# First attention's value products of two head groups at once on four 64x64 quadrants

## What is computed

```python
def _L0_attn_ref(x, q_weight, v_weight, out_w, out_b):
    q = jnp.einsum('tbm,mhd->tbhd', x, q_weight)
    q_sq = jnp.einsum('tbhd,tbhd->tbh', q, q)
    squared_dist = q_sq[:, None] + q_sq[None, :] - 2.0 * jnp.einsum('tbhd,sbhd->tsbh', q, q)
    attn_weights = jax.nn.softmax(-squared_dist * inv_sqrt_d, axis=1)
    A = jnp.einsum('mhd,nhd->hmn', q_weight, q_weight) * inv_sqrt_d
    XA = jnp.einsum('tbm,hmn->tbhn', x, A)
    PXA = jnp.einsum('tsbh,sbhm->tbhm', attn_weights, XA)
    PXAV = jnp.einsum('tbhm,mhd->tbhd', PXA, v_weight).reshape(x.shape[0], x.shape[1], -1)
    return PXAV @ out_w.T + out_b
...
x = x + _L0_attn_ref(_layernorm(x, axis=-1), ...)
x = x + _L0_ffn_ref(_layernorm(x, axis=-1), ...)
```

## Time and profile before

| what | us |
|---|---|
| median of 3 runs (570.55 to 576.7) | 572.35 |
| profiled execution, whole time | 571.84 |
| profiled execution, span of the core | 570.1 |
| PE busy in the span | 563.5 |
| DVE, POOL, ACT busy | 342.5, 230.2, 204.9 |

### The profile page before, as it was taken

How to read it: one execution, slowest core, us unless ns; L and a number is a source line. 1 busy time by engine, 2 the same in 40 slices (tenths; PEclk the granted TensorE clock), 3 DMA queues, 4 the chain that set the end, 5 groups by cost and what they waited for, 6 DMA issues and landing times.

```text
span 570.1 us, 11756 instructions
## 1 busy us (share of the span) xinstructions
PE 563.5 (99%) x5017; PEld 484.4 (85%) x5019; DVE 342.5 (60%) x386; ACT 204.9 (36%) x296; POOL 230.2 (40%) x182
## 2 busy tenths in 40 slices
PE   9999999999999999999999899999999999999997
PEld 6989898898989989898778898978888888888886
DVE  4878672736637265562687467476585447867741
ACT  4543443505335250442562361423341122434220
POOL 2399995674727557368035001103335443000000
PEclk9999999999999999999999999999999999999999
DMA  8463534241222323105240420206923222699501
GB/s 309 144 220 104 180 127 156 75 156 47 100 83 84 146 74 94 62 1 155 59 149 3 160 77 1 75 1 151 229 75 131 91 74 75 186 236 234 156 1 74
DMA packets 24852, 64.91 MB, mean 114 GB/s; under 512 B 2408, under 2 KB 2408, under 8 KB 21872
## 3 DMA queue, kind: packets, MB, share of 16 engines
q1 hardware_dynamic: 24816, 64.38, 36.1%
HBM read 63.20 MB, written 1.18 MB: 113 GB/s over the span
## 4 chain that ended last, share of the span: by engine, by line
PE 89%; DVE 1%; DMA 1%; issue 0%; ACT 0%; POOL 0%
PE ps L333 18%; PE ps L335 18%; PE ps L334 18%; PE ps L864 9%; PE ps L887 3%; PE ps L891 3%; PE ps L879 2%; PE ps L874 2%; PE ps L873 2%; PE ps L878 2%; PE ps L941 2%; PE ps L1187 1%; PE ps L905 1%; DMA raw<-in_ctx 1%; PE ps L912 1%; PE ps L1170 1%
## 5 line engine op out<-in xcount | busy, mean ns | idle before, releaser
L473 POOL TENSOR_TENSOR psum_tmp<-psum_tmp,raw 128x512 f32<-128x512 f32 (+1 forms) x88 | 147.7, 1679 | 28.7 <-DVE lo L1431 20.0
L864 PE MATMUL ps<-hi 128*128 128x256 f32 (+3 forms) x416 | 129.2, 312 | 0.1
L1431 DVE TENSOR_TENSOR lo<-raw,hi 128x2048 fp32r<-128x2048 f32 (+1 forms) x29 | 62.3, 2166 | 30.9 <-ACT hi L545 30.8
L864 PEld LDWEIGHTS ps<-hi 128*128 128x128 f32 (+1 forms) x416 | 78.2, 188 | 1.7 <-DVE lo L1431 0.4
L333 PE MATMUL ps<-hi,gh 128*128 128x512 f32 x192 | 75.5, 393 | 0.0
L335 PE MATMUL ps<-hi,gl 128*128 128x512 f32 x192 | 74.8, 390 | 0.0
L334 PE MATMUL ps<-lo,gh 128*128 128x512 f32 x192 | 74.7, 389 | 0.0
L526 POOL TENSOR_TENSOR sx<-sx,raw 128x512 f32<-128x512 f32 x32 | 41.1, 1290 | 78.2 <-DVE raw L1779 78.1
L749 ACT ACTIVATE hi<-raw 128x2048 fp32r<-128x2048 f32 x14 | 26.8, 1916 | 87.2 <-PE ps L335 77.6
L333 PE MATMUL ps<-wvh,gh 128*128 128x512 f32 x128 | 51.1, 400 | 0.0
L335 PE MATMUL ps<-wvh,gl 128*128 128x512 f32 x128 | 50.0, 391 | 0.0
(11 more groups left out here) (229 smaller groups left out, 1168.2 us busy)
## 6 DMA issues: line engine op xcount, KB each, us to landing
raw<-in_ctx SPq DMA_DIRECT2D x23, 1024.0 KB, 4.9
raw<-in_ve SPq DMA_DIRECT2D x8, 1024.0 KB, 5.3
raw<-in_oe SPq DMA_DIRECT2D x8, 1024.0 KB, 7.1
wk<-gm_rows SPq DMA_DIRECT2D x8, 512.0 KB, 9.7
g<-gm_rows SPq DMA_DIRECT2D x8, 512.0 KB, 10.6
raw<-in_ctx SPq DMA_DIRECT2D x8, 130.0 KB
xres<-in_x SPq DMA_DIRECT2D x1, 1024.0 KB, 9.7
mb<-in_WqT SPq DMA_DIRECT2D x1, 1024.0 KB, 13.6
```

The lines of the kernel that those rows point to most:

```text
L473: pool.tensor_tensor(psum_tmp[0:k, :], (raw[:, 0, :] if t == 1 else psum_tmp[0:k, :]), raw[0:k, t, :], ALU.add).then_inc(ctx_sum, 1)
L864: pe.matmul(dst, hi[0:kk, t, cols], x, start=start and opens, stop=stop and closes, skip_group_check=True)
L1431: dve.tensor_tensor(lo[0:k, r, :], raw[0:k, r, :], hi[0:k, r, :].bitcast(F32), ALU.subtract).then_inc(ctx_lo, 1)
```

## The change

`near_values(n, gs)` now does the head groups 2n and 2n+1 together. The odd one's output goes to the other 64 rows, so that it uses the two quadrants off the diagonal. Its rows are therefore swapped by halves through `near_norm`, and its transposes multiply by a permutation, `swapped`, in place of the identity. POOL makes `swapped` in three instructions. `near_norm(0)` takes its two banks one after the other. Three orders are rewritten: PE's products, ACT's fourth values ahead of its fourth exponential, and DVE's two low parts for the next layer, which go behind `near_low(3)`.

```diff
@@ POOL, behind masks()
+            pool.memset(swapped[:, :], 0.0).then_inc(swap_set, 1)
+            for n, base in enumerate((S, -S)):
+                pool.wait_ge(swap_set, n + 1)
+                pool.affine_select(out=swapped[:, :], in_=swapped[:, :], compare_op=ALU.not_equal, fill=1.0, base=base,
+                                   pattern=[[-1, P]], channel_multiplier=1).then_inc(swap_set, 1)
@@ ACT
             nearness(2)
+            values_out(3)
             nearness(3)
-            values_out(3)
@@ PE
-            def near_values(c, gs=range(NG)):
-                pe.wait_ge(d_exp, c + 1)
+            def near_values(n, gs):
+                pe.wait_ge(d_exp, 2 * n + 2)
...
-                    pe.wait_ge(vv_done, g + 1 if c != 1 or g < 2 else NG)
+                    pe.wait_ge(vv_done, g + 1 if g < 2 else NG)
                     for j in range(4):
...
+                        for turned in range(2):
+                            c = 2 * n + turned
+                            for cg in range(2):
+                                row = slice(S * cg, S * cg + S)
+                                out_row = S * (1 - cg if turned else cg)
+                                col = (g % 2) * 4 + j
+                                mm = pe.matmul(bank[num_bank(c, g)][out_row:out_row + S, col * (D1 + 1):(col + 1) * (D1 + 1)],
...
-                    mm.then_inc(nv_mm, 1)
+                    mm.then_inc(nv_mm, 2)
...
-                    mm = pe.transpose(turn_bank(c)[:, tok], mb[:, c, tok], ident[:, :])
+                    mm = pe.transpose(turn_bank(c)[:, tok], mb[:, c, tok], (ident, swapped)[c % 2][:, :])
@@ DVE
-            w_low(W_Q2, 0)
             near_norm(0)
             near_norm(1)
             near_norm(2)
             near_low(0)
             near_low(1)
-            dve.wait_ge(wg_hi_done, 2)
-            dve.tensor_tensor(wg_lo, wg_raw, wg_hi.bitcast(F32), ALU.subtract).then_inc(wg_lo_done, 1)
             near_norm(3)
             near_low(2)
             near_low(3)
+            w_low(W_Q2, 0)
+            dve.wait_ge(wg_hi_done, 2)
+            dve.tensor_tensor(wg_lo, wg_raw, wg_hi.bitcast(F32), ALU.subtract).then_inc(wg_lo_done, 1)
```

More of the change, by code:

```diff
@@ L86, in perceiver_block @@
         identb = sb("identb", [P, P], BF16)
+        swapped = sb("swapped", [P, P])
         headmask = sb("headmask", [P, P])
@@ L151, in perceiver_block @@
         ld_w = [sem("ld_w0"), sem("ld_w1")]
-        consts, bfconst, blank_set = sem("consts"), sem("bfconst"), sem("blank_set")
+        consts, bfconst, blank_set, swap_set = (sem(s) for s in ("consts", "bfconst", "blank_set", "swap_set"))
         c_mm, c_done, ld_bq = sem("c_mm"), sem("c_done"), sem("ld_bq")
@@ L1171, in head_values @@
                 mm.then_inc(vv_mm, 1)
-            def near_values(c, gs=range(NG)):
-                pe.wait_ge(d_exp, c + 1)
-                if c == 0:
+            def near_values(n, gs):
+                pe.wait_ge(d_exp, 2 * n + 2)
+                if n == 0:
                     pe.wait_ge(vv_ones, 1)
                     pe.wait_ge(row_done, 2)
-                if c == 2:
+                else:
                     pe.wait_ge(d_add, 8)
                 for g in gs:
-                    pe.wait_ge(vv_done, g + 1 if c != 1 or g < 2 else NG)
+                    pe.wait_ge(vv_done, g + 1 if g < 2 else NG)
@@ L1183, in near_values @@
                     for j in range(4):
[L1184 to L1189, removed]
+                        for turned in range(2):
[5 more added lines that the diff above has]
+                                mm = pe.matmul(bank[num_bank(c, g)][out_row:out_row + S, col * (D1 + 1):(col + 1) * (D1 + 1)],
+                                               near_heads_of(c)[row, j * 2 * P + g * S:j * 2 * P + g * S + S],
+                                               vv[row, g, 4 * c + j, :], start=True, stop=True, skip_group_check=True)
@@ L1190, in near_values @@
                 if gs.stop == NG:
-                    mm.then_inc(nv_mm, 1)
+                    mm.then_inc(nv_mm, 2)
             def turn_values(c):
                 pe.wait_ge(nv_done, c + 1)
+                if c == 1:
+                    pe.wait_ge(swap_set, 3)
                 for g in range(NG):
                     tok = slice(g * P, (g + 1) * P)
-                    mm = pe.transpose(turn_bank(c)[:, tok], mb[:, c, tok], ident[:, :])
+                    mm = pe.transpose(turn_bank(c)[:, tok], mb[:, c, tok], (ident, swapped)[c % 2][:, :])
@@ L1210, in _ @@
             near_values(0, range(0, 2))
+            head_values(3)
+            near_values(0, range(2, NG))
             near_values(1, range(0, 2))
-            head_values(3)
-            near_values(2, range(0, 2))
-            near_values(0, range(2, NG))
             near_values(1, range(2, NG))
-            near_values(2, range(2, NG))
             turn_values(0)
             turn_values(1)
-            near_values(3)
             def transpose_e(u):
@@ L1669, in near_norm @@
                 dve.wait_ge(nv_mm, c + 1)
[L1670 to L1674, removed]
+                parts_of = range(2) if c == 0 else range(1)
+                count = 2 // len(parts_of)
+                steps = 2 if c == 0 else c + 2
+                for n in parts_of:
+                    heads = ps[:, num_bank(c, 2 * n):num_bank(c, 2 * n) + count, 0:8 * (D1 + 1)].rearrange("p k (h d) -> p k h d", d=D1 + 1)
+                    per_head = rowrec[:, c, :].rearrange("p (k h) -> p k h", k=2)[:, n:n + count, :]
+                    dve.reciprocal(per_head, heads[:, :, :, D1]).then_inc(d_rec, 1)
+                    dve.wait_ge(d_rec, n + 1 if c == 0 else steps)
+                    ins = dve.tensor_tensor(mb[:, c, :].rearrange("p (k h d) -> p k h d", k=2, d=D1)[:, n:n + count, :, :], heads[:, :, :, 0:D1],
+                                            per_head.unsqueeze(3).broadcast_to([P, count, 8, D1]), ALU.mult)
+                ins.then_inc(nv_done, 1)
             def near_low(c):
```

## The result

| | before | changed |
|---|---|---|
| median of 20 runs, us | 573.01 | 575.74 |
| lowest and highest, us | 570.55, 579.05 | 571.48, 579.21 (of 19) |
| profiled execution, whole time and span, us | 571.84, 570.1 | 578.5, 576.8 |
| granted clock of PE over that span, mean | 1.00 | 0.99 |

The ratio is 1.0045 (95% interval 1.0023 to 1.0066): slower by about half a per cent. The forecast was 571.1, with a range up to 574.2, so it missed, and its sign too. One of the 20 changed runs took 3156 us: the ratio and the highest time leave it out, the median has it in and is 575.63 without it.

What follows compares the result with a forecast made beforehand. PE was taken as the bound, busy 563.5 of 570.1 us. Of 3.6 us saved on the value products, new waits left a lead of 0.68: 571.84 less 0.7 gives 571.1 us, range 568.9 to 574.2.

Steps and rivals of the forecast that it cites:

- Points 1 and 2: First two quarters of the value products: the first ends at 334.08, the second waits 0.68 us for the values' copy.
- the first rival: Value products: the four quadrants do not overlap, 31 ns per instruction, nothing saved, 574.7 us; chance 0.11.
- The copy's wait: Ahead of the second quarter of value products: PE newly waits 0.68 us for ScalarE's copy of the last values.
- The gross saving: Value products: 256 instructions at 17.0 ns instead of 31.1, 3.6 us.
- Point 3: Last two quarters of value products: the fourth exponential costs PE nothing, 0.1 us to spare; both end at 339.12.
- Points 4 to 8: Norms to transposes: out_part(0) waits 0.96 us, PE gets 1.83 ahead, VectorE only 0.32, transposes wait about 0.9.
- The waits at the transposes: Layer norm's transposes ahead of the second layer: PE waits about 0.9 us for VectorE's second tile.
- The last rival: Ahead of the change, at L335: the 1.6 us stall repeats or is lost, 572.7 or 569.5 us; chance 0.06.

Runs made afterwards that it cites:

- e1: The changed kernel run again with no edit, against the kernel before: 575.49 us, ratio 1.0086.
- e3: The changed kernel with 96 more PE instructions at its start (four large and 53 very small warm-up products for nine): 573.81 us, ratio 1.0052 to the kernel before.
- e7: The changed kernel with the load of W_K2 held until the second row of norms is done: 575.32 us, ratio 1.0035 to the kernel before.
- e13: The changed kernel with W_K2's load later and the last values computed ahead of the first quarter of products: 572.19 us, ratio 0.9993 to the kernel before.
- e5: The changed kernel with 96 more PE records at its start, eight of nine large warm-up products kept: 572.99 us, ratio 0.9998 to the kernel before.
- e9: The kernel before with only the load of W_K2 made later: 570.80 us, ratio 0.9945 to the kernel before.
- e11: The changed kernel with W_K2's load later and 14 extra products on zeros filling PE's pauses: 574.52 us, ratio 1.0023 to the kernel before.
- e12: The changed kernel with W_K2's load later, 12 filling products and VectorE's low parts at their old places: 576.99 us, ratio 1.0061 to the kernel before.
- e14: The changed kernel with W_K2's load later, last values first, low parts back, first expert's load held: 571.00 us, ratio 0.9988 to the kernel before.

## Why the prediction was wrong

**Points 1 and 2 held.** 64 instructions took 1.07 us (forecast 1.09), 16.7 ns each against 31, so the four quadrants do overlap and the first rival is out. What the prediction drew for that rival from the Trainium skill's page TensorE: Matmul & The Clock Gate, Part 3 (The mechanism), that four quadrants with two row groups go no faster than two, does not hold in these products either. The copy's wait was 0.78 (0.68). The gross saving was put at 3.6 us, all 256 instructions at 31.1 ns; the earlier trace rows have 7.83 us for them, which makes it 3.5. The walk through the points goes by the rows and is not touched by this.

**Point 3 failed: "Both quarters end at 339.12".** It counted 128 instructions at 17 ns behind the second quarter and asked for nothing but semaphores. PE's instructions have to arrive, too. In e1, the run at full clock, the quarters ended 8.04 us after the first began (333.77 to 341.81), not 6.13, and 1.83 of the difference of 1.91 is the stall for the piece at record 7445. From the first product to the queries e1 took 24.16 us, before 22.74, and the forecast says 22.06. The fourth exponential, of which point 3 was afraid, made no wait.

**Points 4 to 8 held, about 2 us late.** out_part waited 1.07 us (0.96); VectorE went from `near_low(3)` without a break to the residual, which came 16.88 us after the first product in e1 and 15.18 in before: 1.70 later, where 0.32 earlier was forecast. The waits at the transposes were 0.5 in all (0.9). In e3, where the stall was 0.48, the first product to the queries took 22.80 us, 22.74 before; less the stall that is 22.3, against 22.06 by the forecast.

**The clock was taken as 1.00 throughout**, because the profiled execution showed nothing else. The runs shown already reached 576.7; the scatter of 6 us was put down as scatter, and it was the clock's falls. With the change they came in 21 of 23 runs instead of 44 of 110. By the sessions' medians a run with a fall takes 4.4 us more (571.0 against some 575.4). An estimate from these numbers is (0.91 - 0.40) x 4.4 = 2.2 of the 2.7 us between the two medians. It leaves +0.5 where the forecast had -0.7; that this is the stall is argued, from the traces, since only two runs of the changed kernel were at full clock (571.48 and 574.19). **The last rival was near**: a stall that "a changed instruction stream might repeat". It was the right place to look, but priced as chance, at 0.06, and without its mechanism, which makes it repeat where the products use up a piece before the next one has come.

What stays open: which pauses bring the clock down. No order by the longest or the summed pause of the traces fits: e7 (0.97, 0.78, 0.62 and 0.65) fell in 8 of 10, e13 (1.02, 1.84 and 1.07) in 4 of 10, e5 (0.76, 0.78 and 1.06) in none, and e1's traced execution had 0.71, 0.78, 1.83 and 1.07 without a fall. e9 and e11 show that the falls go away with the pauses: with the stall near 324 us in before, with work put into them in the changed stretch. How many or how long they must be is not shown, and neither is where e11's other runs lost their 2 us.

## What to carry to other kernels

When a change makes many short instructions run faster, ask how fast they can be delivered: here 256 records (a product instruction is two, with its weight load) take 3.6 to 3.9 us to come, so less than about 15 ns per record, kept up over more than one piece, was not to be had. A stall marked "issue" with no releaser, at a fixed record number, is a sign of such a piece. A large load moving at that time makes it longer, and one wait on SyncE can move the load away; but look where it moves to, since here it held up a later piece. And read the spread of the runs before the forecast: a spread of 1% on one core was here a second mode, and a change that adds pauses can move runs into it.

## What the runs showed of the hardware that I had not expected

- Between 320 and 365 us the stalls without a releaser fall on a grid of 256 PE records (6677, 7189, 7445, 7701) in every kernel traced. Where PE stalled with no 1 MB load in the way, 3.3 us (e11: 335.56 to 338.85) to 4.1 us (e13: 334.62 to 338.72) had passed from PE's start in one piece, or from the end of a semaphore's wait among its first ten records, to the first record of the next.
- A 1 MB load in flight made that 6.0 us (e12: 336.72 to 342.75). The piece then moved in the load's last microsecond: 323.23 and 323.41 in before, 331.48 and 331.77 in e14, 340.23 and 340.46 in e12 (start of the packet, end of the load).
- The granted clock went to 0.5 for 3.4 to 10 us at a time around pauses of 0.5 to 3.3 us with small products between them; in none of the traced falls was PE idle for longer.
- Eight products on one pair of quadrants followed by eight on the other run at 20 to 22 ns an instruction, one pair alone at 31, all four in turn at 16.7.
